# Decoder layer on one core: second weight folding moved in the planned order, the load of x split, expert registers read one by one

## The chip, the cores and the metric

The kernel runs on one core of one Trainium2 chip. The metric is the device time in microseconds of one launch, and the time of a kernel is the median of its runs. The core has five engines with queues of their own: PE (TensorE), DVE (VectorE), ACT (ScalarE), POOL (GpSimd) and SP, which here only issues DMAs. Each engine takes its own instructions in the order in which they are written, so an instruction that waits holds up all that stand behind it on the same engine.

## The reference

One decoder layer over x of 8 batches x 112 positions x 256:

```python
x = x + self_attention(layernorm(x))            # 16 heads of 16, causal, with biases
x = x + cross_attention(layernorm(x), ctx, mask)  # ctx of 375 positions, 16 heads of 16
x = x + experts(layernorm(x))                    # top 2 of 8 experts, gated slot attention
```

In the cross attention each head's values go through the small matrix Wv (16x16) and the result through Wo (256x256), `out @ Wo.T + bo`. Since nothing nonlinear stands between the two, the kernel multiplies them once (this is the "second folding" of the title, `fo` = blocks of Wv times Wo) and applies `fo` alone.
The expert layer picks two experts for each position, sorts the positions by expert into tiles of 128 rows, applies the expert's weights for keys, forget gates and values, runs a scan over chunks of 64 slots per head and brings the rows back in order.

## The kernel before

The work is cut into *stages*, each a few instructions on one engine: `("stats", 0, b)`, `("qk", b)`, `("S", unit)` and so on. `Plan` (from L126) holds for each stage a cost, a rank, what it needs and an earliest time `at`, and simulates a greedy run: of all stages that are ready it takes the one with the smallest key, first the time at which it could start (not before `at`, and not before the engine is free plus a small slack), then the rank. That gives the order of the stages on each engine and the PSUM banks. This is done before the program is built; on the chip the engines follow the fixed order and synchronise by semaphores. `COST`, `BIAS`, `SLACK`, `LAG` and `LANDS` are the planner's numbers.

The order of the work:

- **Head.** SP issues the loads one after another (L717 to L739): x of batches 0 and 1 (`l_x0`), the identity, the query weights, biases, key weights, the causal masks (`l_cm`), value weights, bias rows, x of batches 2 and 3, and so on to `wvo` and a row of biases (both `l_wo`, L732 and L733). PE multiplies zeros five times (L781, `pT`) while it waits. The layer norm of a batch is `norm`: DVE takes the statistics (`stats`, L1184 and L1186), POOL the root (L1687 and L1689), DVE normalises (`xn`, L1193), PE transposes (`xnT`), ACT copies it out of PSUM. In the plan, `stats` of batches 0 and 1 have `at=3.5` (L182).
- **Self attention** of a batch is `qk`, `v`, and two *units* of 8 heads; **cross attention** is four units per batch. A unit is S (scores), max, mT (transpose of the maxima), q2, st (scores again, transposed), exp, pv, oT. The six units of batches 0 to 2 come first, then units of cross attention with those of self attention three batches ahead between them. `oproj 0` closes the self attention of a batch with `wos`, `oproj 1` the cross attention with `fo`.
- **Folding.** `combine 0` makes `bdq` for the cross queries. `combine 1` (the second folding) makes `fo`: two products on PE and one copy on DVE (L1235). PE waits for `l_wo` ahead of it (L828); its earliest time in the plan is `at=19.5` (L176). On the chip only `oproj 1` of batch 0 waits for `fo` (L917), in the plan also `oproj 0` (L271).
- **Experts.** Batches form two groups (0 to 4, 5 to 7) with 16 and 13 tiles. `tables` ends with the expert offset of each tile in `eti` (DVE, L1137). The stage `regs` of a group (L949) waits for it and reads all offsets of the group into registers of PE's sequencer with one load (L951). Each tile then has x (transposes), `pkf` (keys and gates, four instructions on PE), `pvx` (values, four), and its softplus and sigmoid on ACT and DVE. `pkf` and `pvx` find the weights in `wm` by the tile's register. The scan over the batches follows.

Of the kernel before, what the change touches and what calls it, by code (L numbers as in the profile page):

```python
# [4 lines left out]
NB, S, D, NK = 8, 112, 256, 375  # L5
# [8 lines left out]
GNT = [(2 * c + NE * 127) // 128 for c in GCAP]  # L14
GT0 = [sum(GNT[:g]) for g in range(NG)]
GBASE = [NE * sum(GCAP[:g]) for g in range(NG)]
NT = sum(GNT)
ZROW = NE * S * NB
TG = [g for g in range(NG) for _ in range(GNT[g])]
# [31 lines left out]
        "pvc": (0.62, 0.78), "pvs": (0.43, 0.59), "pvx": (0.86, 1.03), "qTx": (0.76, 0.92),  # L51
        "qgT": (0.19, 0.36), "qk": (1.79, 1.95), "regs": (0.5, 0.5), "siT": (0.19, 0.36),
        "stc": (1.43, 1.59), "sts": (0.98, 1.14), "stx": (0.89, 1.07), "tm": (0.48, 0.65),
# [36 lines left out]
    "T": {"G": -67, "Sc": -161, "Ss": -925, "cb": 292, "fT": 212, "fo": 935, "inf": -17, "kTx": -152,  # L90
          "logits": -273, "onT0": -97, "oproj0": -37, "oproj1": 169, "pkf": 342, "pvs": 1037, "pvx": 181,
# [8 lines left out]
}  # L100
SLACK = {"T": 0.3, "V": 0.1, "A": 0, "P": 0.15, "S": 0}
# [24 lines left out]
class Plan:  # L126
# [38 lines left out]
    def build(self):  # L165
        add = self.add
# [14 lines left out]
        for b in range(NB):  # L181
            self.norm(0, b, 100 * b - 260, [], at=3.5 if b < 2 else 11.5 if b < 4 else 45.0)  # L182
            r = 100 * b - 240
# [1699 lines left out]
```

## Time and profile before

| | |
|---|---|
| median of 3 runs | 462.94 us |
| lowest, highest | 459.88 us, 474.88 us |
| the profiled execution | 463.49 us |
| its span, first to last instruction | 461.7 us |
| PE busy (matmul) | 432.3 us, 94% |
| DVE, ACT, POOL busy | 306.3, 244.8, 179.7 us |
| mean granted clock of PE | 0.985 of full speed |

The span is what the trace shows from the first to the last instruction; 1.8 us of the profiled execution's time lie around it. "Granted clock" is the share of TensorE's full clock: 1.00 is 2.4 GHz, 0.50 is 1.2 GHz. In the lines of the profile the time in square brackets is how long the engine stood idle before the instruction, and behind the arrow is what ended that.

### The profile page before, as it was taken

What the parts mean: (1) busy time and instruction counts of PE and PEld (TensorE: products, weight loads), DVE (VectorE), ACT (ScalarE), POOL (GpSimd) and SP (SyncE); (2) the same over time, 40 slices, a digit from 0 to 9 for tenths busy, and PEclk for the clock granted to TensorE, in tenths of its full rate; (3) what the DMA queues carried; (4) which work ended last, traced back from release to release, by engine and by line L of the source; (5) the groups of instructions that cost most, each with busy time, mean ns of one, the idle gap of its engine ahead of it and who ended that gap; (6) DMA issues with size and microseconds to landing.
All of it is one profiled execution on the core that took longest, in us unless ns stands there. A gap on an engine that the chain in (4) does not pass through costs nothing.

```text
span 461.7 us, 12854 instructions
## 1 busy us (share of the span) xinstructions
PE 432.3 (94%) x4632; PEld 317.0 (69%) x4632; DVE 306.3 (66%) x1034; ACT 244.8 (53%) x663; POOL 179.7 (39%) x240
## 2 busy tenths in 40 slices
PE   8879899999999899997979999899899999999997
PEld 6656576867667577664646666565578766988885
DVE  4736757487577577676786559995366675876663
ACT  5123233425443434443536778787675876777652
POOL 5451033132732752145332268626543214444320
PEclk9989979999999899999999999999999999999999
DMA  7848323544436335011210244445723332121202
GB/s 205 170 128 289 122 81 115 158 139 111 135 136 156 123 106 155 3 35 41 55 38 25 92 143 134 152 161 176 227 62 103 105 110 104 65 75 53 66 11 61
DMA packets 23918, 51.07 MB, mean 111 GB/s; under 512 B 3105, under 2 KB 13546, under 8 KB 23858
## 3 DMA queue, kind: packets, MB, share of 16 engines
q1 hardware_dynamic: 20018, 38.02, 26.5%
q0 software_dynamic: 3440, 11.15, 8.9%
q10 hardware_dynamic: 400, 1.10, 0.8%
q8 instruction: 39, 0.64, 0.6%
q14 instruction: 21, 0.17, 0.1%
HBM read 28.75 MB, written 21.50 MB: 109 GB/s over the span
## 4 chain that ended last, share of the span: by engine, by line
PE 76%; DMA 7%; DVE 5%; ACT 3%; issue 3%; another core or an unknown queue 3%; SPq 2%; ACTq 1%; POOL 0%; DVEq 0%; POOLq 0%
PE ps L781 67%; PE ps L784 9%; DMA rw_sb<-in_rows 3%; DMA kv<-kd_d,idk 3%; DVE jnk L1259 1%; ACT pT L1529 1%; DMA kd_d<-kd 1%; ACT u L1586 0%; ACT u L1584 0%; SPq L714 0%; DVE kd L1390 0%; DVE kd L1384 0%; ACT u L1588 0%; ACTq L1498 0%
## 5 line engine op out<-in xcount | busy, mean ns | idle before, releaser
L1529 ACT ACTIVATE pT<-ps 125x672 f32<-125x672 f32 (+1 forms) x96 | 60.6, 666 | 93.0 <-PE ps L781 84.1
L781 PE MATMUL ps<-wm,xsT 128*128 x232 | 83.4, 492 | 0.5 <-ACT xsT L1579 0.5
L1259 DVE CUSTOM_DVE_ANT_0 jnk<-ps,mkb 112x375 bf16<-112x375 f32 x128 | 63.6, 544 | 21.7 <-PE ps L781 21.7
L781 PEld LDWEIGHTS ps<-wm,xsT 128*128 128x128 f32 x232 | 41.0, 190 | 24.3 <-issue 21.6
L1758 POOL DMA_INDIRECT xs<-xs_d,idg x29 | 28.9, 997 | 29.8 <-PE ps L784 22.1
L781 PE MATMUL ps<-cxT,cqT 32*112 32x375 f32 x256 | 28.7, 518 | 7.3 <-ACT pT L1529 3.1
L781 PE MATMUL ps<-q,cxT 32*125 32x112 f32 x768 | 30.7, 291 | 0.0
L781 PEld LDWEIGHTS ps<-q,cxT 32*125 32x125 f32 x768 | 24.9, 190 | 7.8 <-issue 7.6
L1803 POOL TENSOR_TENSOR qg<-okb,dc 112x256 f32<-112x256 f32 x16 | 11.8, 736 | 42.4 <-ACT okb L1627 42.3
L1264 DVE TENSOR_REDUCE mxz<-ps 112x2 f32<-112x224 f32 x64 | 21.0, 383 | 10.3 <-PE ps L781 10.3
L1384 DVE SCALAR_TENSOR_TENSOR kd<-ps,u 128x512 f32<-128x512 f32 x29 | 19.9, 685 | 9.0 <-ACT u L1588 7.4
L781 PE MATMUL ps<-pT,cxp 125*32 125x112 f32 x768 | 25.7, 267 | 0.0
L1627 ACT ACTIVATE okb<-okb,sm 112x64 f32<-112x64 f32 x64 | 21.4, 338 | 8.1 <-DVE sm L1436 8.1
L781 PE MATMUL ps<-mkT,idb 125*125 125x336 bf16 x128 | 24.6, 315 | 0.9 <-DVE xbo L1284 0.6
L1584 ACT ACTIVATE u<-ps 128x512 f32<-128x512 f32 x29 | 17.3, 596 | 14.4 <-PE ps L781 13.7
L1741 POOL DMA_INDIRECT xs_d<-y,idu x16 | 15.8, 990 | 21.2 <-DVE idu L1347 18.0
L1687 POOL TENSOR_SCALAR st<-st 112x1 f32<-112x1 f32 x16 | 3.8, 235 | 49.2 <-DVE st L1186 49.2
L781 PEld LDWEIGHTS ps<-pT,cxp 125*32 125x32 f32 x768 | 17.8, 111 | 7.3 <-ACT pT L1529 2.7
L781 PEld LDWEIGHTS ps<-mkT,idb 125*125 125x125 bf16 x128 | 16.0, 139 | 8.4 <-issue 3.1
L1796 POOL DMA_INDIRECT kv<-kd_d,idk x16 | 15.3, 955 | 15.8 <-issue 6.9
L1722 POOL TENSOR_SCALAR mkb<-mki 112x375 bf16<-112x375 int32 x8 | 12.2, 1524 | 20.2 <-DVE mxz L1259 14.1
L781 PEld LDWEIGHTS ps<-cxT,cqT 32*112 32x112 f32 x256 | 9.8, 173 | 14.9 <-ACT pT L1529 7.7
(242 smaller groups left out, 1059.2 us busy)
## 6 DMA issues: line engine op xcount, KB each, us to landing
kd_d<-kd SPq DMA_DIRECT2D x29, 384.0 KB
xs_d<-xs SPq DMA_DIRECT2D x8, 896.0 KB, 4.2
wm<-in_wmoe SPq DMA_DIRECT2D x8, 768.0 KB, 4.3
cxT<-in_ctxT SPq DMA_DIRECT2D x32, 93.8 KB, 3.4
cx<-in_ctx SPq DMA_DIRECT2D x8, 375.0 KB
mki<-in_mask SPq DMA_DIRECT2D x8, 164.1 KB
mti<-in_maskT SPq DMA_DIRECT2D x8, 164.1 KB
out<-xbo SPq DMA_DIRECT2D x8, 112.0 KB, 1.8
```

The source lines that it names most:

```text
L781: return e.matmul(o, l, r, start=start, stop=stop)
L784: return e.transpose(o, i, ident[0:n, 0:n])
L1259: e.tensor_tensor_reduce(jnk[:, j % 2, :], ps[0:S, bk, 0:NK], mkb[:, b % 2, :], 1.0, -3e38, ALU.add, ALU.max, mxz[:, n % 2, 0, c:c + 1]).t ...
L1264: e.tensor_reduce(mxz[:, n % 2, :, :].rearrange("p i m -> p (i m)")[:, c:c + 113:112], ps[0:S, bk, 0:2 * S].rearrange("p (g n) -> p g n", ...
L1384: e.scalar_tensor_tensor(kd[:, t % RD, 0:512], ps[:, slot["pkf", t][0], 0:512], 0.0, u[:, r, :], ALU.min, ALU.subtract).then_inc(v_ls, 1)
L1529: e.activation(pT[0:w, n % RP, 2 * i:2 * i + 2, 0:m], ps[0:w, b0:b1 + 1:b1 - b0, 0:m], ACT.Exp).then_inc(a_pT, 1)
L1584: e.activation(u[:, r, :], ps[:, slot["pkf", t][0], 0:512], ACT.Abs).then_inc(a_sp, 1)
L1627: last = e.activation(w, w, ACT.Exp, bias=s4[:, h:h + 1], accum_out=s4[:, 4 + h:5 + h])
L1722: e.tensor_scalar(mkb[:, b % 2, :], mki[:, b % 2, :], 0.0, -1e20, ALU.is_equal, ALU.mult).then_inc(p_mkb, 1)
L1741: e.indirect_dma_start(out=xs_d.ap(), out_offset=bass.IndirectOffsetOnAxis(ap=idu[:, k, b:b + 1], axis=0), in_=y[:, b % RY, :], in_offset= ...
L1758: e.indirect_dma_start(out=xs[:, t % RX, :], out_offset=None, in_=xs_d.ap(), in_offset=bass.IndirectOffsetOnAxis(ap=idg[:, t:t + 1], axis= ...
L1796: e.indirect_dma_start(out=kv[:, t % RK, :], out_offset=None, in_=kd_d[g].ap(), in_offset=bass.IndirectOffsetOnAxis(ap=idk[:, b, j:j + 1], ...
```

## The change

Four things, in the program's text:

1. The stage `combine 1` may start at 42 instead of 19.5 of the plan's time and with a later rank, and in the plan `oproj 0` no longer needs it. Its instructions are the same.
2. The load of x for batches 0 and 1 is split. Batch 0 is loaded first, batch 1 behind the key weights, on the semaphore of the causal masks `l_cm`, which now has to reach 32. `stats` of batch 1 and the copies of the masks wait for 32.
3. `regs` reads two offsets instead of 16 or 13. Behind each `pkf` of tile t a load of one register reads the offset of tile t+2, while that is of the same group (25 such loads).
4. The planner's costs, biases and slacks are replaced, the earliest times of `pad` and `mkb` (POOL) are later, and so every engine's order is planned anew. The earliest time of `stats` (L182) is not changed.

```diff
@@ COST, "T" (PE), those that change
-  "mTs": (0.2, 0.41)  "okx0": (0.75, 0.91) "ovx0": (0.75, 0.91) "pkf": (1.72, 1.88) "pvc": (0.62, 0.78)
-  "pvx": (0.86, 1.03) "regs": (0.5, 0.5)   "stc": (1.43, 1.59)  "x": (0.22, 0.38)
+  "mTs": (0.3, 0.41)  "okx0": (0.8, 0.95)  "ovx0": (0.8, 0.95)  "pkf": (1.76, 1.89) "pvc": (0.66, 0.79)
+  "pvx": (0.89, 1.03) "regs": (0.6, 0.6)   "stc": (1.48, 1.62)  "x": (0.25, 0.38)
@@ COST, "V" (DVE)
-  "msk3": (0.62, 0.7)  "msk2": (0.75, 0.83) "msk1": (1.0, 1.08)  "split": (0.36, 0.45)
+  "msk3": (0.62, 0.71) "msk2": (0.79, 0.87) "msk1": (0.98, 1.06) "split": (0.98, 1.04)
@@ BIAS: all replaced
-SLACK = {"T": 0.3, "V": 0.1, "A": 0, "P": 0.15, "S": 0}
+SLACK = {"T": 0.3, "V": 0.2, "A": 0.15, "P": 0.2, "S": 0}
@@ LANDS
-    "gk": 2.8
+    "gk": 3.2
@@ build
-        add("T", ("combine", 1), 0.9, -230, release=("V", ("combine", 1)), at=19.5)
+        add("T", ("combine", 1), 0.9, -40, release=("V", ("combine", 1)), at=42.0)
@@ pad, mkb
-                at=18.0 if b == 0 else 25.0)
+                at=26.0 if b == 0 else 30.0)
-                + ld("ldmask", 2), at=15.0 if b == 0 else 23.0)
+                + ld("ldmask", 2), at=19.0 if b == 0 else 29.0)
@@ output
-        add("T", ("oproj", k, b), 0.9, r, [("A", ("onT", k, b)), ("V", ("combine", 1))], ("V", ("oproj", k, b)), at=17.0)
+        add("T", ("oproj", k, b), 0.9, r, [("A", ("onT", k, b))] + ([("V", ("combine", 1))] if k else []), ("V", ("oproj", k, b)), at=17.0)
@@ sync
-            e.dma_start(xbo[:, 0:2, :], x[:, 0:2, :]).then_inc(l_x0, 16)
+            e.dma_start(xbo[:, 0:1, :], x[:, 0:1, :]).then_inc(l_x0, 16)
             e.dma_start(cst[:, 0:128], consts[:, 0:128]).then_inc(l_id, 16)
             e.dma_start(wqk[:, 0, :, :], watt[:, 0, :, :]).then_inc(l_wq, 16)
             e.dma_start(bqk[:, :], bself[:, 0:8]).then_inc(l_bqk, 16)
             e.dma_start(wqk[:, 1, :, :], watt[:, 1, :, :]).then_inc(l_wk, 16)
+            e.dma_start(xbo[:, 1:2, :], x[:, 1:2, :]).then_inc(l_cm, 16)
             e.dma_start(cst[:, C_CB:C_CB + 224], consts[:, C_CB:C_CB + 224]).then_inc(l_cm, 16)
@@ tensor
-                    e.load(regs[GT0[b]:GT0[b] + GNT[b]], eti[0:1, GT0[b]:GT0[b] + GNT[b]])
+                    e.load(regs[GT0[b]:GT0[b] + 2], eti[0:1, GT0[b]:GT0[b] + 2])
...
                         last.then_inc(t_pkf, 1)
+                        if t + 2 < NT and TG[t + 2] == TG[t]:
+                            e.load(regs[t + 2:t + 3], eti[0:1, t + 2:t + 3])
@@ vector
-                    if k == 0 and b in (0, 2, 4):
-                        e.wait_ge((l_x0, l_x, l_late)[min(b // 2, 2)], (16, 16, 48)[min(b // 2, 2)])
+                    if k == 0 and b in (0, 1, 2, 4):
+                        e.wait_ge((l_x0, l_cm, l_x, l_x, l_late)[min(b, 4)], (16, 32, 16, 16, 48)[min(b, 4)])
...
-                    e.wait_ge(l_cm, 16)
+                    e.wait_ge(l_cm, 32)
                     e.tensor_copy(cmb[:, :, :], cst[0:S, C_CB:C_CB + S].unsqueeze(1).to_broadcast([S, 2, S])
```

## Rows read from the trace of the kernel before

**Rows 1.** The page: busy time of the engines; the chain that ended last.
```profile
PE 432.3 (94%) x4632; PEld 317.0 (69%) x4632; DVE 306.3 (66%) x1034; ACT 244.8 (53%) x663; POOL 179.7 (39%) x240
PE 76%; DMA 7%; DVE 5%; ACT 3%; issue 3%; another core or an unknown queue 3%; SPq 2%; ACTq 1%; POOL 0%; DVEq 0%; POOLq 0%
```

**Rows 2.** Waits of PE, the longest in total: us, times, longest.
```profile
PE ps L781 <- DMA rw_sb<-in_rows: 3.3, 1, 3.3
```

**Rows 3.** Stretches: us, busy time of each engine (instructions), granted clock, DMA share, GB/s.
```profile
6.90:22.10 15.20, 13.88 (x148) 11.48 (x148) 10.79 (x34) 2.40 (x4) 6.77 (x10) 1.00 0.90 181
22.10:25.40 3.30, 0.04 (x1) 0.07 (x1) 0.39 (x1) 0.68 (x2) 1.52 (x2) 1.00 0.67 179
26.90:30.40 3.50, 3.50 (x36) 2.49 (x37) 1.82 (x5) 1.34 (x3) 1.83 (x2) 0.51 0.33 124
54.20:57.70 3.50, 1.75 (x25) 0.99 (x21) 3.39 (x16) 0.00 (x0) 0.80 (x2) 0.99 0.04 14
57.70:64.40 6.70, 6.33 (x45) 5.30 (x45) 4.64 (x17) 2.44 (x5) 3.38 (x8) 0.50 0.42 139
200.00:246.00 46.00, 38.66 (x577) 26.40 (x575) 33.29 (x149) 20.16 (x49) 17.63 (x21) 1.00 0.13 34
320.00:345.00 25.00, 22.06 (x142) 16.14 (x141) 12.41 (x28) 18.65 (x59) 13.29 (x16) 1.00 0.51 161
```

**Rows 4.** Timeline around the second folding: start us, us, engine, line, what.
```profile
21.67 0.41 PE L784 MATMUL ps<-cst,mxz 112*128 112x112 f32 x2
...
22.18 0.39 DVE L1243 TENSOR_TENSOR q<-qkT,ps 128x224 f32<-128x224 f32 x1 [0.99 <-PE ps L784]
...
23.73 0.82 POOL L1716 COPY cxp<-cx 125x768 f32<-125x768 f32 x1 [3.84 <-DMA cx<-in_ctx]
...
25.36 1.10 PE L781 MATMUL ps<-wvo 128*128 128x256 f32 x4 [3.29 <-DMA rw_sb<-in_rows]
```

**Rows 5.** Timeline of the head.
```profile
1.26 4.63 PE L781 MATMUL ps<-pT 125*125 125x256 f32 x10 [1.26 <-DVE pT L1195]
...
3.05 0.43 SPq L722 DMA_DIRECT2D cst<-in_consts  x1
3.44 0.43 DVE L1184 BATCH_NORM_STATS2 st<-xbo 112x6 f32<-112x256 f32 x1 [2.23 <-DMA xbo<-in_x]
3.52 0.43 SPq L723 DMA_DIRECT2D wv<-in_watt  x1
...
4.00 0.39 DVE L1184 BATCH_NORM_STATS2 st<-xbo 112x6 f32<-112x256 f32 x1
...
4.43 0.18 DVE L1186 BATCH_NORM_AGGREGATE st<-st 112x2 f32<-112x6 f32 x1
...
5.20 0.41 DVE L1193 TENSOR_SCALAR xn<-xbo,st 112x256 f32<-112x256 f32 x1 [0.59 <-POOL st L1689]
...
6.86 2.01 PE L781 MATMUL ps<-xnT,wqk 128*128 128x112 f32 x16 [0.49 <-ACT xnT L1512]
```

**Rows 6.** DMA issues: engine, count, KB, us from issue to landing.
```profile
cst<-in_consts SPq DMA_DIRECT2D x1, 112.0 KB, 3.7
```

**Rows 7.** The two register loads: ns min/median/max, first and last start.
```profile
L951 PEldq TENSOR_LOAD <-eti x2: 1117/1208/1298, 237.1 to 291.0; - x2
```

**Rows 8.** Timeline around the two register loads.
```profile
237.12 0.41 PE L784 MATMUL ps<-cst,y 112*128 112x112 f32 x2
...
237.75 0.08 DVE L1259 DVE_READ_ACCUMULATOR2_ANT mxz<- 112x1 f32 x1
...
238.50 0.14 PEld L784 LDWEIGHTS ps<-cst,mxz 112*128 112x128 f32 x1 [1.18 <-DVE mxz L1259]
...
292.32 0.99 PE L781 MATMUL ps<-W,yq 112*128 112x224 f32 x4 [1.53 <-issue]
```

**Rows 9.** Timeline of one tile's pkf and pvx, eight matmuls, and a weight load in it.
```profile
293.15 2.75 PE L781 MATMUL ps<-wm,xsT 128*128 x8
...
294.01 0.19 PEld L781 LDWEIGHTS ps<-wm,xsT 128*128 128x128 f32 x1 [0.24 <-issue]
```

More of the change, by code:

```diff
@@ L47 @@
         "kTx": (0.19, 0.36), "kp": (1.77, 1.95), "logits": (0.9, 1.06), "mTc": (0.15, 0.31),
[1 row of a table removed]
[1 row of a table added]
         "okx1": (1.19, 1.35), "onT0": (0.19, 0.35), "onT1": (0.2, 0.38), "oproj0": (0.87, 1.03),
[1 row of a table removed]
-        "pvc": (0.62, 0.78), "pvs": (0.43, 0.59), "pvx": (0.86, 1.03), "qTx": (0.76, 0.92),
-        "qgT": (0.19, 0.36), "qk": (1.79, 1.95), "regs": (0.5, 0.5), "siT": (0.19, 0.36),
-        "stc": (1.43, 1.59), "sts": (0.98, 1.14), "stx": (0.89, 1.07), "tm": (0.48, 0.65),
[2 rows of a table removed]
[1 row of a table added]
+        "pvc": (0.66, 0.79), "pvs": (0.43, 0.59), "pvx": (0.89, 1.03), "qTx": (0.76, 0.92),
+        "qgT": (0.19, 0.36), "qk": (1.79, 1.95), "regs": (0.6, 0.6), "siT": (0.19, 0.36),
+        "stc": (1.48, 1.62), "sts": (0.98, 1.14), "stx": (0.89, 1.07), "tm": (0.48, 0.65),
[2 rows of a table added]
         "am": (0.53, 0.62), "combine0": (0.34, 0.42), "combine1": (0.6, 0.69), "consts": (0.5, 0.58),
@@ L89 @@
 BIAS = {
-    "T": {"G": -67, "Sc": -161, "Ss": -925, "cb": 292, "fT": 212, "fo": 935, "inf": -17, "kTx": -152,
-          "logits": -273, "onT0": -97, "oproj0": -37, "oproj1": 169, "pkf": 342, "pvs": 1037, "pvx": 181,
[7 rows of a table removed]
+    "T": {"G": -5, "R": 118, "Sc": -228, "Ss": -774, "cb": 167, "fT": 291, "fo": 1376, "inf": 89, "kTx": -303,
+          "logits": 183, "nrm1": -300, "okx0": 127, "onT0": -150, "onT1": -365, "oproj0": -132, "oproj1": 60,
+          "ovx0": 93, "ovx1": -281, "pkf": 406, "pvs": 892, "pvx": 285, "qTx": 322, "siT": 302, "stx": -219,
+          "tm": -194, "v": 80, "x": -202, "xnT1": 105},
+    "V": {"kk": -858, "ls": -130, "maxc": -143, "maxs": -264, "msk0": 228, "nrm0": -169, "oo": -175,
+          "oproj0": -221, "pick": 79, "rwa": 254, "rwb": 45, "split": 298, "stats1": -296, "stats2": 427,
+          "tab0": 154, "tab14": 48, "tab3": 21, "tab5": 243, "tb4": 172, "xn0": 404},
+    "A": {"es": -328, "expc": 318, "exps": 337, "oTs": 226, "qgT": -609, "siT": 38, "x": 41, "xnT1": 222,
+          "yT": 311},
+    "P": {"gx": 166, "qTf": 147},
     "S": {},
 }
-SLACK = {"T": 0.3, "V": 0.1, "A": 0, "P": 0.15, "S": 0}
+SLACK = {"T": 0.3, "V": 0.2, "A": 0.15, "P": 0.2, "S": 0}
 def kind(stage):
@@ L129 @@
            "VT": 0.146, "VV": 0.0, "PA": 0.1, "PT": 0.15}
-    LANDS = {"later": 8.0, "zero": 8.0, "gx": 2.6, "gk": 2.8, "scatter": 3.0, "kd": 2.5, "ldmask": 4.0, "ldctx": 3.0, "ldctxT": 4.0}
+    LANDS = {"later": 8.0, "zero": 8.0, "gx": 2.6, "gk": 3.2, "scatter": 3.0, "kd": 2.5, "ldmask": 4.0, "ldctx": 3.0, "ldctxT": 4.0}
     UNIT = ("S", "max", "mT", "q2", "st", "exp", "pv", "oT")
```

15 rows, old and new, of tables (BIAS, COST) are left out of this document.

## The prediction

> **What bounds the kernel now.** I read the page first: PE is busy 94% of the span and holds 76% of the chain that ended last [rows 1]. So the time is PE's work plus what PE stands idle, 461.7 - 432.3 = 29.4 us, plus what it loses at the low clock. Then I asked who keeps PE waiting: the longest entry is a single wait of 3.3 us for the row of biases that arrives with `wvo` [rows 2]. The timeline shows its place: PE ends a transpose at 22.08, and the folding starts at 25.36 [rows 4]. Last I read the stretches for the granted clock. In 22.1 to 25.4 PE does nothing, and from 26.9 to 30.4 it is busy without a break at 0.51, which is 1.2 GHz for nearly all of it; the same after 54.2 to 57.7, where PE is busy for 1.75 of 3.5 us, and then runs at 0.50 until 64.4 [rows 3]. An idle PE is thus paid twice in this kernel.
>
> **The change, part by part.** All sums go against the profiled execution: span 461.7, time 463.49, so 1.8 us lie around. It is 0.55 above the median of 462.94, and the three runs shown span 15 us.
>
> *The folding moves.* The wait of 3.29 us at 25.36 goes [rows 4]. What is late next on PE is the second transposed score product, which needs `q2`: DVE ends it at 22.57 [rows 4]. So PE still stands some 22.57 - 22.08 = 0.5 us, call it 0.4 with a bias product put ahead. Gain 3.29 - 0.4 = 2.9. The folding's own 1.10 us on PE is moved, not removed: 0. Its copy goes to DVE where DVE has idle time, 0. `oproj 1` of batch 0, its only user, comes well behind 42 us (the cross units of batch 0 must end first), so there is no new wait. The 3.5 us at the low clock behind the stall did the work of 1.75; if no stall, no low clock: gain 1.7 (bounds 0 and 1.75).
>
> *x is split.* This is the part that the text does not show at once. The first landing can only be earlier, but the order on DVE decides. `stats` of batch 1 keeps its earliest time 3.5 in the plan. The planner ends `stats` of batch 0 at about 4.1 and finds `xn` of batch 0 ready only about 1 us later, behind POOL's root, so `stats` of batch 1 goes between them, as it does before (4.00, then `xn` at 5.20 [rows 5]). On the chip it will now wait there for `l_cm` at 32, and `xn` of batch 0 stands behind it on DVE, and with it the transposes, ACT's copy and `qk`: all of PE's head. When is 32? Before, the masks were issued at 3.05 and landed 3.7 later [rows 5, 6], at 6.75. Now one more load is issued ahead of them, a step of 3.52 - 3.05 = 0.47 [rows 5]; the bytes up to there are the same. Landing between 6.75 and 7.2, I take 7.0. Then `stats` and aggregate, 4.61 - 4.00 = 0.61 [rows 5], and `xn` starts at 7.6 instead of 5.20. Loss 2.4 (bounds 2.2 and 2.7). PE is busy for 13.88 of the 15.20 us that follow [rows 3], so next to nothing takes it up. POOL's biases and root stand behind the same statistics, but are needed only after `qk`. `qk` began 6.86 - 5.20 = 1.66 behind the start of `xn` [rows 5], so it will begin at 9.3. PE's warm-up products end at 5.9 [rows 5], and from there to 9.3 PE has only two transposes to do. That is about as long as in the stall that was followed by 3.5 us at the low clock [rows 3]. I expect the same here: loss 1.5 (bounds 0 and 1.75). Without this order, x alone first would bring at most a few tenths, since PE's warm-up products and the POOL root stand there anyway.
>
> *The registers.* The loads of 16 and 13 registers take 1.298 and 1.117 us [rows 7], that is 0.060 per register and 0.333 for the load: 0.45 for two, 0.39 for one, by that line. In group 1 PE waits 1.53 us [rows 8] and the load is what ends it, so 1.117 - 0.453 = 0.66 is gained. In group 0 the load starts at 237.1 and runs its 1.298 to 238.4, and PE goes on at 238.50. The maxima that PE needs there are done at 237.83 [rows 8], which PE sees some 0.1 to 0.2 later, at 238.0: gain 0.45. Together 1.1. Against it stand 25 new loads. Do they lie beside matmuls? The load of group 0 starts at 237.1, when the transposes ahead of it have only begun (237.12 for 0.41 us), so the sequencer executes it while the array works [rows 7, 8]. In a tile the weight loads of `pkf` take 0.19 and stand idle for 0.24 between [rows 9]: the array sets the pace, one matmul in 0.43 us, and the sequencer waits. The new load stands behind four such matmuls, so it has at least the last one's 0.43 as cover for its 0.39. I take 0; bounds 0 and 25 x 0.39 = 9.8.
> The Trainium skill (DMA: Bandwidth & Descriptors, Latency and other measured facts) speaks against this part: it gives a register load a floor of about 600 ns and advises to bundle them. By that, with the same cover, each would stick out by 0.17 and the 25 would cost 4.3 us, which would make my sum 464.5; the two long loads here agree with either a floor or a line, and no row shows a short one.
>
> *POOL's later times.* `pad` waited 3.84 us for ctx with the addition to x behind it [rows 4]; later it waits less. Nothing on PE hung on it: 0.
>
> *Planned anew.* The trace of before cannot show the new order. What it could win is PE's idle time in 200 to 246, 46.00 - 38.66 = 7.3, in 320 to 345, 25.00 - 22.06 = 2.9, and half of the 6.7 us at the low clock, 3.35 [rows 3]: 13.6 in all. What it could lose is a new stall like the old one, 3.3 + 1.7 = 5.0 each. A stall like the old one, which the plan could not see, shows that an order can be worse on the chip than in the plan; new prices may fit better or not, and no row settles it. I choose a tenth of what is open: a gain of 1.4 (bounds: a gain of 13.6, a loss of 10 for two stalls).
>
> Sum: -2.9 - 1.7 + 2.4 + 1.5 - 1.1 + 0 - 1.4 = -3.2. Time 463.5 - 3.2 = 460.3 us.
>
> **The rivals.**
> 1. *The head is not lost*: `xn` of batch 0 comes before the wait, or the mask lands at once. Nothing in the rows speaks for it; the unchanged `at` speaks against. 460.3 - 2.4 - 1.5 = 456.4. This would be the change doing all that it says.
> 2. *The register loads stand in the open* (the other side): each load delays the values' weights by up to its whole 0.39, 460.3 + 9.8 = 470.1. It decides the sign from 3.2 / 25 = 0.13 us per load. For it: the load is on the queue that bounds the kernel, and the sequencer runs ahead only while no semaphore holds it. Against: the load stands ahead of the waits of `pvx`, beneath four matmuls of `pkf`, 4 x 0.43 = 1.7 us [rows 9].
> 3. *The new order makes stalls*: one to two of 5.0 us (a wait and the low clock behind it), 465 to 470.
> 4. *The new order closes gaps*: two thirds of the 13.6, so 9 instead of 1.4: 452.7.
> 5. *The loads stand half in the open*: the line through two long loads may give a short one too little, and the weight loads of `pvx` have to pass in the same 0.43 of cover. Half of 0.39 each, 25 x 0.195 = 4.9: 465.2. No row speaks against it but that PE's array sets the pace there. The floor of the Trainium skill (the page and section above) would come out near this.
>
> **How the numbers follow.** My case, within 3.5 us of 460.3, 0.48; head not lost 0.08; loads fully open 0.05, half open 0.09; new stalls 0.14; gaps closed 0.16. The range leaves out the lower half of the last and the upper end of rivals 2 and 3: 453 to 467.5. A change under 2% of 462.94, 9.3 us, is about what a measurement of this kernel can tell from none. Faster by over 2% means below 453.7: most of rival 4 sits around it, with a little of rival 1 on top of a good order, 0.12. Slower by over 2% means above 472.2: rival 2 with a stall on top, 0.05. The rest, 0.83, lies within.
>
> **What would show each step.** In the changed profile DVE should wait near 4 to 7 us ahead of the second `stats`, and the first `qk` on PE should start near 9.3 instead of 6.86, followed by some 3.4 us at 0.50 of the clock. At 22 to 30 no wait for the bias row and full clock. Two loads of about 0.45 us, 25 of about 0.39, and `pkf` with `pvx` still 2.75 us for eight matmuls; 3.1 would be rival 2. If PE's busy time falls by about 1 us and its idle time by about 2, the sum holds. The prediction fails if the order in the middle is much better or worse than before, which no row could tell.

## The result and the profile after

| | before | changed |
|---|---|---|
| median (10 runs each) | 462.97 us | 466.07 us |
| lowest, highest | 459.88, 474.88 us | 465.10, 469.75 us |
| ratio, 95% interval | | 1.0075 (1.0045 to 1.0105) |
| the profiled execution | 463.49 us | 465.27 us |
| its span | 461.7 us | 463.5 us |

The change costs 3.1 us. I had forecast a gain of 2.6 against the median. Both lie inside 2%, and 466.07 is inside the range, but the sign is wrong. The ratios and their intervals, here and below, use only executions within 1.5% of the fastest of their kernel, the medians use all of them, so a ratio can differ a little from the quotient of the medians.

The lines of the changed kernel come in the order of the prediction. First the page (busy time; shares of the chain that ended last) and PE's longest waits (us in total, times, longest):

```profile
PE 433.2 (93%) x4632; PEld 315.2 (68%) x4632; DVE 314.2 (68%) x1034; ACT 245.7 (53%) x663; POOL 179.8 (39%) x240
PE 78%; DVE 7%; ACT 6%; issue 4%; POOL 2%; another core or an unknown queue 1%; DMA 1%; ACTq 1%; SPq 1%; DVEq 0%; POOLq 0%
...
PE ps L783 <- DVE mb L1329: 6.4, 1, 6.4
...
PE ps L786 <- DVE xn L1197: 2.2, 1, 2.2
```

PE is busy for 0.9 us more than before and idle for 463.5 - 433.2 = 30.3 us instead of 29.4. The wait for the bias row [rows 2] is not in the list any more. In its place stands a wait twice as long, on DVE, that no part of the prediction names. DVE is busy for 314.2 us instead of 306.3 [rows 1] with the same 1034 instructions: 7.9 us more for the same work, which is the first hint (6.3 of them are one instruction, below).

The stretches (columns as in [rows 3]):

```profile
8.90:12.40 3.50, 3.49 (x17) 3.50 (x18) 0.69 (x4) 1.43 (x1) 2.28 (x6) 0.51 1.09 226
22.10:25.40 3.30, 3.30 (x47) 2.95 (x40) 1.59 (x5) 0.00 (x0) 1.44 (x2) 1.00 0.65 193
155.80:162.60 6.80, 3.51 (x22) 2.69 (x26) 5.92 (x19) 1.53 (x5) 2.95 (x5) 0.50 0.00 1
200.00:246.00 46.00, 41.48 (x640) 28.48 (x637) 33.77 (x146) 20.41 (x47) 18.75 (x23) 1.00 0.16 40
320.00:345.00 25.00, 24.57 (x146) 17.01 (x146) 14.88 (x35) 20.06 (x54) 13.55 (x16) 1.00 0.64 198
```

22.1 to 25.4, idle before, is now busy throughout. In 200 to 246 PE is idle for 4.5 us instead of 7.3, in 320 to 345 for 0.4 instead of 2.9 [rows 3] (the same clock times are not quite the same work). So the new order does close gaps. Against it stand the low clock at 8.9 and the stretch from 155.8.

The head on the timeline, where [rows 5] had the statistics of batch 1 at 4.00, `xn` at 5.20 and `qk` at 6.86 for 2.01 us:

```profile
6.94 0.43 DVE L1188 BATCH_NORM_STATS2 st<-xbo 112x6 f32<-112x256 f32 x1 [3.16 <-DMA cst<-in_consts]
7.50 0.38 DVE L1197 TENSOR_SCALAR xn<-xbo,st 112x256 f32<-112x256 f32 x1
8.03 0.38 PE L786 MATMUL ps<-cst,xn 112*128 112x112 f32 x2 [2.23 <-DVE xn L1197]
8.91 3.64 PE L783 MATMUL ps<-xnT,wqk 128*128 128x112 f32 x16 [0.49 <-ACT xnT L1516]
```

DVE stood 3.16 us for the masks' semaphore with `xn` of batch 0 behind it, as forecast, and `qk` begins 2.05 us later and takes 1.63 longer.

The register loads (ns min/median/max, first and last start), the pairs and the single ones:

```profile
L953 PEldq TENSOR_LOAD <-eti x2: 556/642/727, 240.7 to 291.6; - x2
L971 PEldq TENSOR_LOAD <-eti x25: 297/309/782, 253.2 to 380.1; - x25
```

And the new wait, on the timeline, with all instructions that make the mask `mk` of the chosen experts (ns min/median/max) under it:

```profile
151.46 7.07 POOL L1713 TENSOR_SCALAR wm<-wm,nwc 128x768 f32<-128x768 f32 x8
151.91 0.17 DVE L1309 MAX8 k<-tk 112x8 f32<-112x8 f32 x1
152.11 6.45 DVE L1311 TENSOR_TENSOR mk<-tk,k 112x16 f32<-112x16 f32 x1
...
159.09 0.32 PE L783 MATMUL ps<-mb,ltb 112*112 112x8 bf16 x2 [6.41 <-DVE mb L1329]
...
L1311 DVE TENSOR_TENSOR mk<-tk,k x8: 174/175/6445, 132.6 to 282.5; 112x16 f32<-112x16 f32 x8
```

One DVE instruction of 0.175 us took 6.45. It reads two operands in SBUF, began 0.65 us behind POOL's row of eight instructions on the experts' weights (the stage `fold`: each weight matrix times the layer norm's scale), and ended 0.03 us behind the end of that row, 151.46 + 7.07 = 158.53. The `MAX8` just ahead of it, with one operand in SBUF, began inside the same row and was not slowed. In before, the same eight lie at 156.8 and 164.7 and meet no `mk`, of which the longest took 0.33 us; but an `xn` that DVE began at 165.01, inside the last two, took 0.73 us instead of 0.40. Behind the gap PE runs at the low clock until 162.6: 3.51 us busy at 0.50, which costs half of that, 1.8. (The expectations below take 3.4 for it, half of the whole stretch of 6.8; but 3.3 us of that stretch is PE standing, already counted in the 6.4.)

This is a rule that I could have used: the Trainium skill (SBUF — State Buffer, section "SBUF: two separate sides") says that a VectorE instruction with two SBUF inputs and a GpSimd instruction that reads SBUF take the same pair of ports as an exclusive lock, for a whole instruction. The trace agrees on who blocks whom. By a lock of one instruction `mk` would have waited until the first of POOL's eight ended, at 152.37, so for 0.26 us and never for more than the 0.9 that one takes; here it took 6.45. Set 1 has both behaviours.

### The profile page after: what moved, and what is told of

Its sections match the earlier page's. It is cut to its first block, busy times and chain, and to the rows that moved or that the text cites. A ratio compares the mean times of both kernels' runs of the same rounds, so it can differ in the third digit from the quotient of the medians.

```text
span 463.5 us, 12880 instructions
## 1 busy us (share of the span) xinstructions
PE 433.2 (93%) x4632; PEld 315.2 (68%) x4632; DVE 314.2 (68%) x1034; ACT 245.7 (53%) x663; POOL 179.8 (39%) x240
## 4 chain that ended last, share of the span: by engine, by line
PE 78%; DVE 7%; ACT 6%; issue 4%; POOL 2%; another core or an unknown queue 1%; DMA 1%; ACTq 1%; SPq 1%; DVEq 0%; POOLq 0%
PE ps L783 69%; PE ps L786 8%; ACT pT L1533 2%; DVE mk L1311 2%; DVE jnk L1263 1%; POOL xs_d L1745 1%; DMA cst<-in_consts 1%; ACTq L1501 0%; POOL xs L1762 0%; ACT sq L1566 0%; POOL Wb L1777 0%; ACT yq L1560 0%; ACT xnT L1516 0%; DVE tk L1303 0%
## 5 line engine op out<-in xcount | busy, mean ns | idle before, releaser
L783 PE MATMUL ps<-wm,xsT 128*128 x232 | 85.1, 497 | 0.7 <-ACT qgT L1644 0.4
L783 PE MATMUL ps<-q,cxT 32*125 32x112 f32 x768 | 29.5, 282 | 0.0
L783 PEld LDWEIGHTS ps<-q,cxT 32*125 32x125 f32 x768 | 23.8, 183 | 7.6 <-issue 7.6
L1544 ACT ACTIVATE oT<-ps 128x112 f32<-128x112 f32 x32 | 8.5, 265 | 20.7 <-PE ps L783 17.8
L783 PE MATMUL ps<-xnT,wqk 128*128 128x112 f32 x128 | 17.7, 296 | 1.4 <-ACT xnT L1516 1.4
```

What stands on the lines that cost most here:

```text
L783: return e.matmul(o, l, r, start=start, stop=stop)
```

## The experiments

Chips differ by more than the change is worth: the kernel before had medians of 454.07, 468.93, 467.04, 453.48 and 463.67 us in the five sets below, each on a chip of its own. So every run is compared within its set, by its ratio to before. Some expectations give times for another chip than the one that the run then got; a time of theirs that was met or missed for that reason shows nothing. In the diffs `+` is put into the kernel named.

**Set 1 (before 454.07): what the row on POOL costs, and the head.**

The row held until DVE has finished the choice of experts of batch 1, the fifth instruction of which is the `mk` that was held, in the changed kernel:

```diff
                 elif what == "fold":
                     e.wait_ge(l_wm[b // 4], (80, 64)[b // 4])
+                    if b == 4:
+                        e.wait_ge(v_top, R_TOP * 2)
```

> The changed kernel, with one wait added on POOL: the fifth folding of expert weights waits until the router's choice of batch 1 is done on DVE. Theory A (POOL's row of eight foldings keeps DVE's product of two SBUF inputs waiting for its 6.45 us): that instruction takes about 0.2 us again, PE's wait of 6.4 us and the 6.8 us at the low clock behind it go, and the span falls by 6.4 + 3.4 = 9.8, to about 454 (time 455.5). Theory B (DVE was held by a landing or by something else that ended by chance at the same time): the instruction stays long, the time stays at 465 to 466. Theory C (the stall only used up slack that the order has later): the instruction is short, but the time falls by less than 4 us.

The row broken up instead, in the changed kernel, each of POOL's instructions waiting for the end of the one ahead:

```diff
                     for i in range(2):
+                        if 2 * b + i:
+                            e.wait_ge(p_fw, 2 * b + i)
                         w = wm[:, b * WC + 768 * i:b * WC + 768 * i + 768]
```

> The changed kernel, each of the sixteen folding instructions on POOL waits for the one before it to have finished; nothing else is moved. Theory A, first form (DVE gets its turn as soon as one POOL instruction ends and the next has not started): DVE's instruction waits for at most one folding, 0.9 us, instead of seven, and the time falls nearly as in the kernel with the fold behind the router, by 8 to 10 us, to 456 to 458. Theory A, second form (POOL keeps its place whatever stands between its instructions): the instruction still takes over 5 us and the time stays at 465 to 467. The Trainium skill (SBUF - State Buffer, SBUF: two separate sides) says that the shared port pair is locked for one whole instruction; by its words the wait should be one folding long even without this edit, which the changed kernel's trace does not show.

Measured: 454.51 us, ratio 1.0056 (1.0018 to 1.0094), and 453.33 us, 1.0014 (0.9982 to 1.0045). The timelines, of the held row first:

```profile
151.49 0.18 DVE L1311 TENSOR_TENSOR mk<-tk,k 112x16 f32<-112x16 f32 x1
151.84 7.50 POOL L1715 TENSOR_SCALAR wm<-wm,nwc 128x768 f32<-128x768 f32 x8 [0.99 <-DVE mk L1311]
153.97 0.64 DVE L1346 TENSOR_TENSOR jk<-mk,pc 112x32 f32<-112x32 f32 x1
154.87 0.62 DVE L1351 CAST idu<-idf 112x4 int32<-112x4 f32 x1
155.39 1.10 DVE L1294 TENSOR_SCALAR y<-xbo,st 112x256 f32<-112x256 f32 x1
```

and of the row broken up:

```profile
151.03 1.99 POOL L1715 TENSOR_SCALAR wm<-wm,nwc 128x768 f32<-128x768 f32 x2
151.67 0.29 DVE L1311 TENSOR_TENSOR mk<-tk,k 112x16 f32<-112x16 f32 x1
153.19 1.91 POOL L1715 TENSOR_SCALAR wm<-wm,nwc 128x768 f32<-128x768 f32 x2 [0.17 <-POOL wm L1715]
```

The second is the telling one. POOL's work lies over the same DVE instruction as in the changed kernel, which starts 0.64 us into the first of the row (0.65 there); only 0.09 to 0.17 us stand between each two of POOL's instructions, 0.10 behind the first. `mk` now takes 0.29 us instead of 6.45: it ends 0.01 behind the end of POOL's first instruction, and the gap of 6.4 is gone. So for `mk` it was the missing break that made the hold so long, not POOL's work beside DVE as such.

The first trace shows that a row without a break does not always hold DVE to its end. Its eight follow each other as closely as in the changed kernel, and later instructions of DVE lie over them: `jk`, with two operands in SBUF like `mk`, took 0.64 us instead of 0.19 and ended 0.04 behind the end of the POOL instruction that it met; the `CAST`, with one operand in SBUF, took 0.62 instead of 0.17; `y` 1.10 instead of 0.41. All six traces with a held row (here and in sets 2 to 5) have these three within 0.03 us. Each waited for one POOL instruction and not for the next. What makes `mk` wait for seven more in all five traces in which it meets the unbroken row is open: it differs from `jk` in operands, in shape and in when it comes (0.65 us into a POOL instruction against 0.30), and no run separates these.

The held row's time is near its forecast, 455.5, only by luck, and the other is under its own, 456 to 458: both were worked out from 465, this chip is faster for before too, and the changed kernel did not run on it.

`xn` of batch 0 put ahead of the statistics of batch 1 in DVE's order, in the changed kernel, and next the load of x as it was before (both keep the rest of the change):

```diff
+        v = order["V"]
+        v.remove(("stats", 0, 1))
+        v.insert(v.index(("xn", 0, 0)) + 1, ("stats", 0, 1))
```

> The changed kernel, on DVE the normalisation of batch 0 is put ahead of the statistics of batch 1; all other orders are the same. Theory A (the head is lost by DVE's order): x of batch 0 lands at 3.1, so the first product of the queries starts near 6.5 instead of 8.9, the 3.4 us at the low clock from 9.0 go, and the span falls by 2.4 + 1.5 = 3.9, to about 459.6 (time 461.4 to 462). Theory B (what the head loses is taken up before 60 us, by ctx and mask landing): the first product starts near 6.5, but the time falls by less than 1.5.

```diff
-            e.dma_start(xbo[:, 0:1, :], x[:, 0:1, :]).then_inc(l_x0, 16)
+            e.dma_start(xbo[:, 0:2, :], x[:, 0:2, :]).then_inc(l_x0, 16)
...
-            e.dma_start(xbo[:, 1:2, :], x[:, 1:2, :]).then_inc(l_cm, 16)
```

> The changed kernel, with x of batches 0 and 1 in one load again and the old waits; the orders are those of the changed kernel. Theory A: the head is as before, the first product of the queries at 6.9, no low clock behind it, and the time falls by 2.0 + 1.7 = 3.7, to about 462. It should be 0.2 to 0.4 slower than the kernel with the normalisation ahead. Theory B (the head's loss is taken up later): less than 1.5 faster than the changed kernel.

Measured: 459.31 us, 1.0170 (1.0098 to 1.0242), and 457.4 us, 1.0113 (1.0057 to 1.0169). Both keep the `mk` of 6.45 us and the gap of 6.41, and both lie above the two kernels without it. That the common load is 1.9 us better than `xn` ahead, where the forecast had it slightly worse, is within the noise: the intervals overlap. `qk` of batch 0 starts at 6.29 and at 6.80 with 2.01 us, so the head is as in before. How far that reaches is seen at the first product of `qk` that ends a gap of 0.41 us in all four traces: 79.85 and 80.04 us in the first two kernels, 78.42 with `xn` ahead, 76.89 with x together. The head's loss is thus 1.4 to 3.2 us at 80 us, and with `xn` ahead part of it is left because PE then waits 0.83 us for the value weights and runs slow at 11.6.

**Set 2 (before 468.93): both mended, and two parts alone in before.** The changed kernel once more; it with the row held and `xn` ahead; before with only the load of x split (change 2); before with only the folding moved, by hand, on PE ahead of the first `xnT` that stands behind `qk` of batch 3 and on DVE behind the `xn` of that one. It is the cross attention's, of batch 0, and not that of batch 3, as the expectation says:

> The changed kernel as it is, to stand beside the mended ones on the same chip: the kernel before ran at 454.1 there and at 463.0 where the change was timed, so the mended kernels can't be set against 466.1. If theory A holds (6.4 us of wait and 3.4 at the low clock by the port, 2.0 + 1.7 by the head), it takes 461 to 464 here: 8 to 10 more than the two kernels with the foldings mended (454.5 and 453.3), 2.5 to 4 more than the two with the head mended (459.3 and 457.4). By the rival (port and head only used up slack) it takes 455 to 458. A ratio to the kernel before of 1.0075, as where it was timed, would mean 457.5.

> The changed kernel with both mends: the second half of the foldings waits for the router's choice of batch 1, and on DVE the normalisation of batch 0 stands ahead of the statistics of batch 1. If the two losses are apart, the gains add: 9 to 10 for the port, 2.5 to 4 for the head, so 449 to 451 where the kernel before takes 454, faster than both kernels. If they overlap, it is no faster than the better one alone, 453.

> The kernel before with the split of x alone; the order is that of before. By my prediction: DVE waits for the masks ahead of the second statistics, the first product of the queries starts at 8.9 to 9.3 and runs at the low clock, and the time is 2.4 + 1.5 = 3.9 longer than before. By the rival that the stall at the second folding takes up the loss (PE waits there for a row of biases that lands at 25.2 whatever PE did before): the stall shrinks from 3.3 to about 1, and the time is 0 to 1 longer.

> The kernel before with the second folding alone moved: on PE ahead of the transposes of the normalised x of batch 3 (in their PSUM bank), its copy on DVE behind that normalisation; all other orders are those of before. By my prediction the wait of 3.3 us and the low clock behind it go: 2.9 + 1.7 = 4.6 shorter than before, 449.5 where before takes 454. By the rival (self attention waits for its own landings or for DVE there, so PE's gap only moves): less than 1.5 shorter.

| | median | ratio, interval | span |
|---|---|---|---|
| changed again | 467.78 | 1.0036 (0.9995 to 1.0078) | 465.6 |
| row held, `xn` ahead | 460.25 | 0.9887 (0.9850 to 0.9924) | 456.4 |
| before, x split | 466.36 | 0.9987 (0.9938 to 1.0035) | 464.2 |
| before, folding late | 463.91 | 0.9912 (0.9856 to 0.9968) | 461.7 |

The two mends turn the changed kernel from no gain into a clear one, 7.5 us in the medians. PE's 4632 instructions stand in the same order in both, so their traces, of one chip, can be compared instruction by instruction: the changed kernel is 2.2 us behind from 44 us on until `mk`, 8.5 behind after the gap and 9.2 at the end. So the head cost 2.2 us against `xn` ahead (whose first `qk` took 3.73 us, so that the slow rate is in both), and the stall 7.0 against a held row, less than the 6.4 + 3.4 of theory A and than the 6.4 + 1.8 read above: behind the held row PE waits 1.7 us for `y`, which the stall had hidden. By its ratio, 1.0036, the changed kernel lies where the rival of its expectation had it (455 to 458 for 454, 1.002 to 1.009) and not where theory A had it (461 to 464, 1.015 to 1.022); but both took over the time of before from another chip, and the pair on this chip speaks for the theory. The folding alone gains 468.93 x 0.0088 = 4.1 us, against 4.6 forecast; PE's longest gap up to 40 us, behind its warm-up, is 0.96 us in its trace (3.29 in [rows 4]). The move by hand has a small cost of its own, 0.79 us that PE waits at 42.4 for the folding's bank.

Splitting x in before cost nothing, and that refutes a sentence of mine. Its timeline:

```profile
8.40 0.43 DVE L1185 BATCH_NORM_STATS2 st<-xbo 112x6 f32<-112x256 f32 x1 [4.51 <-DMA cst<-in_consts]
9.49 0.60 PE L785 MATMUL ps<-cst,xn 112*128 112x112 f32 x2 [3.79 <-DVE xn L1194]
10.58 3.73 PE L782 MATMUL ps<-xnT,wqk 128*128 128x112 f32 x16 [0.49 <-ACT xnT L1513]
24.29 1.93 PE L782 MATMUL ps<-xnT,wqk 128*128 128x112 f32 x15
```

PE stood 3.79 us in the head and began `qk` at 10.58, later still than in the changed kernel. But there is no gap at 25 any more: PE arrives late at a stall whose end is set by a landing, and the landing takes the loss up.

**Set 3 (before 467.04): the loads alone, two parts together, the order alone.** Before with single register loads (change 3); before with x split and the folding late; the changed kernel with x together and two long register loads, which leaves the new order with its late folding; the changed kernel with x together and the row held:

> The kernel before with one part alone: two offsets are read in each register stage and one behind each pkf; order and loads of x as before. If the loads lie beneath matmuls, the extra time behind the last matmul of pkf, which in the changed kernel summed to 1.4 us over 29 tiles against 0.3, cancels the 1.1 us that the two long loads gave: ratio 1.000, between 0.997 and 1.003. If they stand half in the open, 4.9 us: ratio 1.010; fully, 9.8 us: 1.02. If the long loads were the whole of it and the short ones free, 0.998.

> The kernel before with two parts: x split and the folding moved behind by hand (the latter alone came out at 0.9912, the former alone at 0.9987). My theory: the split alone cost nothing because the stall for the bias row, whose end is set by a landing, took the head's loss up. With that stall gone the same split should show: 2.2 to 2.7 us of head and up to 1.5 us of low clock, so a ratio of 0.996 to 1.000, and the first gap above 1 us in the trace is that of the head. Rival: something else behind the head takes the loss up as well (the loads of the value weights or of the context), and the ratio stays at 0.991.

> The changed kernel with x loaded together and the registers in two long loads as before, so that only the new order with the later folding is left. From the changed kernel (ratio 1.004 to 1.008) the head comes off, 1.4 to 3.0 us, and the loads change nothing: ratio 0.998 to 1.002. It keeps the gap of 6.4 us near 157 behind the row of eight POOL foldings. The late folding alone gave 0.991, so by this theory the new order itself costs 3 to 5 us beside it. Rival: the new order is no worse than the old one beside the foldings, and the ratio is 0.991 too.

> The changed kernel with x loaded together and with the POOL foldings of the fifth weight and later held until DVE has ended its last instruction with two operands in SBUF ahead of them. The head is then as before and the gap near 157 is gone. With xn put ahead instead of the common load the ratio was 0.9887; the common load was 1.9 us faster than that in the pair without the wait: ratio 0.985, 456.5 us where before takes 463.5. If head and port are not independent (the earlier head only waits longer for a later landing), 0.989 again.

| | median | ratio, interval |
|---|---|---|
| before, single loads | 464.63 | 0.9982 (0.9927 to 1.0037) |
| before, x split, folding late | 465.20 | 0.9985 (0.9924 to 1.0045) |
| order alone | 467.99 | 0.9968 (0.9882 to 1.0055) |
| x together, row held | 457.44 | 0.9817 (0.9758 to 0.9875) |

The single loads cost nothing, which rules out the half-open 1.010 and the open 1.02. Their trace shows both sides: PE's gaps of 1.00 and 1.53 us at the two long loads are 0.44 and 0.97, which is the 1.1 us that was forecast, and the time from `pkf`'s last matmul to the next, beyond its 0.43, sums to 0.3 us over 29 tiles, as in before.

The order alone came out at 0.9968, with an interval that holds the theory (0.998 to 1.002) and its rival (0.991): it decides nothing. Split and late folding together came out where theory put them (0.996 to 1.000), and the trace has the head's gap of 2.21 us and no other above 1.7; but the interval holds 0.991 as well, so this pair decides nothing. The last kernel differs from the order alone by the held row and the register loads. By the ratios it is 0.0151 x 467.04 = 7 us faster, and its trace still has a stall, a second one that no theory named:

```profile
37.84 0.49 POOL L1706 TENSOR_SCALAR wqm<-wqm,nwc 128x264 f32<-128x264 f32 x1 [13.15 <-DMA nwc<-in_bself]
43.08 0.57 POOL L1692 TENSOR_TENSOR st<-st,epow 112x1 f32<-112x1 f32 x1
43.68 0.41 DVE L1196 TENSOR_SCALAR xn<-x,st 112x256 f32<-112x256 f32 x1 [4.68 <-POOL st L1692]
44.24 0.61 PE L785 MATMUL ps<-cst,xn 112*128 112x112 f32 x2 [3.69 <-DVE xn L1196]
```

POOL waits 13.15 us for the vector that scales the router's weights (the stage `foldq`). Behind it in POOL's new order stand a mask, a copy of the context, another mask and the root of the layer norm, which DVE and then PE need. PE stood 3.69 us here and 4.83 in the order alone, whose profiled execution was one of the two longest of its six. In the changed kernel of the first pair the same wait of POOL was 7.39 us and PE did not stand, because the vector landed by 32.6; in these two it landed at 37.7 and 39.0.

**Set 4 (before 453.48): the second stall.** Before again; the last kernel again; it with `foldq` moved behind that root; and that with the row broken up instead of held:

```diff
+        p = order["P"]
+        p.remove(("foldq", 0))
+        p.insert(p.index(("stats", 1, 0)) + 1, ("foldq", 0))
```

> The kernel before, unchanged, for a trace of it from the chip on which the next three run. By every theory the ratio is 1.000. Its trace should show the folding's gap near 25 (3.3 to 4.6 us elsewhere) and the low clock behind it.

> The changed kernel with x loaded together and the later POOL foldings held, a second time (0.9817 before, 0.9758 to 0.9875). There PE stood 3.69 us at 44.2 and ran at the low clock for 6.8 us behind it, because POOL waited 13.15 us for the scale vector of the router weights with the roots of the layer norm behind it; that vector took 16.2 us to land there, 10.5 to 11.9 in the other traces. If it is the chip that makes it land late, the gap may be gone here and the ratio is near 0.975; if it is the common load with the new order, it is there again: 0.982.

> The kernel of the run before it with POOL's scaling of the router weights moved behind the root of the cross attention's first layer norm. My theory of the gap at 44 (POOL's queue held by the landing): the gap goes and the low clock with it, 3.7 + 3.4 = 7 us where the vector lands late, ratio 0.967; where it lands in time, nothing, the ratio of the run before. Rival: the masks on POOL, which stood behind it, or the root itself are late next and the gap only shrinks.

> As the run before it, but the POOL foldings go one by one, each when PE has reached the unit before, instead of being held once. If what matters is only that no row of them lies over a DVE instruction with two operands in SBUF, the two are equal within 0.003. If the held row still delays PE (1.1 us at 159 in its trace), this one is 1 us faster, 0.002.

| | median | ratio, interval | lowest, highest |
|---|---|---|---|
| before again | 454.39 | 1.0012 (0.9980 to 1.0043) | 451.21, 461.00 |
| x together, row held | 453.33 | 1.0003 (0.9971 to 1.0035) | 450.52, 457.83 |
| `foldq` behind the root too | 449.41 | 0.9922 (0.9895 to 0.9949) | 448.15, 450.82 |
| and the row broken up | 450.00 | 0.9928 (0.9897 to 0.9960) | 447.88, 451.55 |

On this chip before is a better kernel: its folding waits less,

```profile
PE ps L781 <- DMA rw_sb<-in_rows: 1.6, 1, 1.6
```

and three pauses of 1.4 to 1.6 us that its other trace has (last section) are missing. There the repeated kernel gains nothing, 1.0003, where both theories of its expectation had a gain (0.975 and 0.982). The better before is part of the reason; how large a part, no run shows.

The kernel with `foldq` moved is 3.9 us faster than the repeated one, and the spread of its runs falls from 7.3 us to 2.7; the forecast was a ratio of 0.967 or no change, and it was neither. What the 3.9 us are is not shown. In the repeated kernel's trace the vector had landed by 32.8 and there is no stall at 44. The two profiled spans differ by 4.8 us all the same, compared instruction by instruction on PE: it is 1.7 behind by the slow rate of the first `qk`, 2.0 by 33 us and still 2.0 until 157; there a low clock adds 1.2, and the last 1.6 come behind 300 us. That in other executions the vector lands late is a reading of the spread; on this chip it can. The move itself does what it should: in the trace of the last kernel the vector landed at 38.6, later than in the execution with the 3.69 us, and POOL's root was not behind it:

```profile
38.34 0.23 POOL L1693 TENSOR_SCALAR st<-st 112x1 f32<-112x1 f32 x1
...
39.32 0.49 POOL L1709 TENSOR_SCALAR wqm<-wqm,nwc 128x264 f32<-128x264 f32 x1
```

PE's longest gap between 34 and 50 us is 0.86 us there. Holding or breaking up the row makes no difference. (The expectation of the last run has POOL wait for PE; as built, each of POOL's instructions waits for the one ahead, as in set 1.)

**Set 5 (before 463.67): what the order is worth.**

> The kernel before with the folding alone moved behind by hand, a second time, beside the run after it. It was 0.9912 where the folding's gap is 3.3 us or more. Where that gap is 1.65 us, as in the last trace of before, the gain is 1.2 to 2.9 us: 0.994 to 0.997.

> The new order with the common load of x, the later POOL foldings held and POOL's scaling of the router weights behind the root, a second time (0.9922 before). Against the run ahead of it this shows what the new order is worth once its own stalls are out: if the order closes gaps (rival 4 of the prediction), this is 2 to 5 us faster, so 0.980 to 0.992; if it does not, both have the same ratio within 0.003.

Measured: the folding late in the old order 461.78 us, 0.9984 (0.9942 to 1.0027); the mended new order 455.95 us, 0.9855 (0.9785 to 0.9925). The first gained a little less than its forecast (0.994 to 0.997), which its interval holds. The intervals are apart, by 5.8 us in the medians. The second kernel also has the register loads, which are worth 0.6 to 1.1 of these, so the order is worth about 5, to within some 4 us by the intervals. The second one's busy line, and POOL's root now ahead of the scaling:

```profile
PE 428.4 (95%) x4632; PEld 311.4 (69%) x4632; DVE 310.0 (69%) x1034; ACT 245.7 (54%) x663; POOL 180.6 (40%) x240
...
37.45 0.23 POOL L1693 TENSOR_SCALAR st<-st 112x1 f32<-112x1 f32 x1 [3.74 <-DVE st L1192]
...
38.43 0.49 POOL L1709 TENSOR_SCALAR wqm<-wqm,nwc 128x264 f32<-128x264 f32 x1
```

PE is busy for 428.4 us with the same 4632 products as the changed kernel's 433.2: the granted clock is 1.00 in its whole span. Its PE has the order of the kernel of set 3 with x together and the row held, and the two traces are level until the stall at 44; then that one is 3.7 us behind, and 5.7 from 53 us on, which is the price of the second stall with its low clock. This kernel beats before in both sets in which it ran; the changed kernel ran in neither, and was 1.0075 and 1.0036 of before where it ran.

## Why the prediction was wrong, point by point

**The step that failed is "Planned anew".** It was forecast at -1.4 us. With the other terms at what they measured, it came out at about +2.8 to +4.1: the folding -4.1 (set 2), the head +2.05 and +1.63, the register loads -0.6 (in the new order, below), together -1.0, and the medians of the first pair are 3.1 apart, so +4.1; the profiled spans, 1.8 apart, give +2.8. This is a remainder, good to a microsecond or two: its terms come from different chips, and the 1.63 of the head may not be the change's (below). In this term are two opposite things, and I had both as rivals but gave the sum to neither. The stalls (rival 3, chance 0.14): one of 6.41 us and the low clock behind it, 3.51 us at 0.50, 1.8: 8.2 us where it stands and 7.0 in the end (set 2), where the prediction had 5.0 for one. The closed gaps (rival 4, 0.16): what is left, some 3 to 4 us; set 5 shows about 5 for the mended order over the late folding alone. A tenth of 13.6 was a number between the two that neither mechanism gives. It should have been a gain of half the open idle time, against the chance of a stall that no plan sees.

Could the stall have been seen? Not its place, which only the new order shows, and not its length, which the held rows of set 1 do not repeat. But its kind could: both engines' instructions stood in the code, POOL's eight in a row were in the trace of before, and the planner has costs for each engine alone and none for two that lie over each other. I had listed PE's waits and never asked what DVE's instructions would meet when they were moved against POOL's.

**The folding: right in the trace, the size on one chip only.** -4.6 forecast, -4.1 measured alone, with an interval of 1.5 to 6.8 us (set 2); the repeat gave 0.7, within -1.3 and 2.7 (set 5), which leaves 4.6 out. The stall is gone in both traces; what is left there is 0.96 us, for ACT's `pT`, and not 0.4 for `q2` (set 2). Its worth would follow how late the bias row lands, 3.3 us of waiting in the first pair, 4.6 on the chip of set 3 and 1.6 on that of set 4; that this is the difference between sets 2 and 5 is not shown, since no trace of before is from those chips.

**The head: right in the trace, wrong in one sentence.** The masks' semaphore was full at 6.94 (forecast 7.0), `xn` at 7.50 (7.6), `qk` at 8.91 (9.3), and its low clock is there, 3.64 us instead of 2.01. But "next to nothing takes it up" is false for before: the folding's stall, whose end is a landing, took all of it up (before with x split, 0.9987). In the sum it counts all the same, because the change takes that stall away. The two terms were not independent, and I had added them as if they were. Also the low rate is not the split's alone: with x loaded together, or `xn` ahead, the sixteen products of `qk` took 2.01 us in ten profiled executions and 3.66 to 3.73 in four; in all six with the split and the old DVE order they took 3.08 to 3.73. In the four the row of the stretch gives the clock as 1.00 all the same (set 4, x together and row held; columns as in [rows 3]):

```profile
6.90:10.30 3.40, 3.40 (x16) 3.40 (x17) 0.64 (x4) 1.43 (x1) 0.23 (x1) 1.00 0.95 283
```

So that these are at the low clock is read from their duration alone, and whether the split made the head slow or only left it no chance is not settled.

**The registers: right, by the trace.** With single loads in the old order (set 3) PE's two gaps are 1.1 us shorter, as forecast, and the 25 loads add nothing that shows. Two registers took 0.556 and 0.727 us where the line of the two long loads gave 0.45. One took 0.297 at least, 0.309 in the middle and 0.782 at most, where it gave 0.39. The loads lie beside matmuls: the time from `pkf`'s last matmul to the next, beyond its 0.43, sums to 1.4 us over 29 tiles in the changed kernel and 0.3 before, and I took the difference for their cost. It is the new order's: with the order alone and no single load the sum is 1.2, with single loads in the old order 0.3. So the 25 cost about 0.2 us in the new order and nothing in the old. In the new order the two gaps at the long loads are 0.86 and 1.08 us, and 0.59 and 0.51 in the changed kernel: 0.8 gained, 0.6 with the 0.2 off. The floor of about 600 ns of the Trainium skill (DMA: Bandwidth & Descriptors, Latency and other measured facts), which I weighed against this part, is not what this chip shows for one register. (The page does not say in so many words to bundle such loads; that was my reading of it.)

**POOL's later times: cost nothing here, but not for the reason given.** "Nothing on PE hung on it" held for `pad`. It did not hold for `foldq`, which in the new order has a mask, the copy of the context and another mask behind it, and then the root; in the old one these three stood ahead of it and only the root behind. That took 3.69 and 4.83 us of PE in set 3. Whether it was the later times of `pad` and `mkb` that turned this round or the new costs, no run shows.

## What to carry to other kernels

When instructions are moved on one engine, look at what they will now lie over on the engines beside them: here a DVE instruction of 0.175 us with two operands in SBUF was held for 6.45 us by an unbroken row of POOL instructions, and 0.1 us between the first two of them was enough to let it through, while others lost 0.4 to 0.7 us each over such a row. The trace shows it as one instruction far longer than its like. A stall whose end is set by a landing hides every loss ahead of it, so taking the stall away can make those losses count, and the two edits must be costed together. A planned order is only as good as its landings: put work that waits for a DMA behind the small work that the critical engine needs, even if the plan has it landing in time.

## What the runs showed of the hardware that was not expected

**A POOL instruction holds DVE, and sometimes the whole row behind it does.** Eight instructions of 0.88 us each held one DVE instruction for the rest of the row (6.45 us, in five traces); with 0.1 us between the first two it waited 0.11 us longer than usual (two traces). Over the same unbroken row, three other DVE instructions waited for one POOL instruction each (0.64, 0.62 and 1.10 us instead of 0.19, 0.17 and 0.41, in six traces), one of them a `CAST` with a single operand in SBUF. `MAX8`, with one, lost nothing inside the row (0.17).

**The chip matters more than the change.** The same kernel had medians from 453.5 to 468.9 us on five chips. Part of it shows in the traces: at the same places of the program PE, DVE and ACT all stand at once for about 1 us on some chips and not on others. The changed kernel's trace has two, which cost PE 1.68 and 2.10 us; the first begins near 178.4:

```profile
178.05 0.38 SPq L702 DMA_DIRECT2D mti<-in_maskT  x1
179.42 0.26 ACT L1544 ACTIVATE oT<-ps 128x112 f32<-128x112 f32 x1 [2.81 <-remote]
...
179.52 0.82 POOL L1720 COPY cxp<-cx 125x768 f32<-125x768 f32 x1 [0.81 <-remote]
```

"remote" is a release that nothing on this core explains. In before there are three such places, 1.40, 1.63 and 1.49 us of PE; both chips on which none of the traces has them are those on which before took 454 us. What they wait for stays open; I made no run on it. Before has three of them and the changed kernel two, 4.5 and 3.8 us of PE, so up to a microsecond of what the new order gains on such a chip may be theirs; in set 5 both kernels have two, of 3.0 and 3.3 us.
